# A routing front written as one pipeline over eight blocks, with its parts in another order on three engines

## The reference, cut to what matters

```python
h = layernorm(x) * (1 + ca) + sa
x = x + ga * mamba_stack(h)                     # 4 layers over (8, 512, 128)
h = layernorm(x) * (1 + cb) + sb
normed = h * rsqrt(mean(h*h) + 1e-8) * norm_weight
shared = relu(normed @ sw1 + sb1) @ sw2 + sb2   # 128 -> 512 -> 128
probs = sigmoid(normed @ router_w.T)            # 8 experts
scores, idx = top_k(probs, 2); w = scores / (sum(scores) + 1e-6)
routed = sum over the two chosen e of w_e * (relu(normed @ ew1[e] + eb1[e]) @ ew2[e] + eb2[e])
out = x + gb * (shared + routed)
```

## Time and the profile before

| | us |
|---|---|
| median of 3 runs | 1139.5 (1137.28 to 1139.51) |
| profiled execution, its own time | 1144.36 |
| its span, first to last instruction | 1142.4 |
| Mamba stage, ends with the last add on POOL | at 793.5 |
| `slot(0)` starts | at 808.00 |
| `slot(7)` starts | at 927.79 |
| first matmuls of the experts (transposes) | at 944.83 |
| experts end, sum and output begin | about 1118 |

### The profile page before, as it was taken

The page is one execution under the profiler, slowest core; times in us unless marked ns, Lnnn a source line. Parts: engine busy times, 40 slices in busy tenths (PEclk is TensorE's granted clock), DMA queues, the critical chain, the costliest instruction groups (busy, mean ns, idle before and its releaser), DMA issues.

```text
span 1142.4 us, 20674 instructions
## 1 busy us (share of the span) xinstructions
PE 995.8 (87%) x6136; PEld 557.6 (49%) x6136; DVE 970.0 (85%) x1801; ACT 864.6 (76%) x1636; POOL 675.6 (59%) x853
## 2 busy tenths in 40 slices
PE   5699999999999999999999999985878767999970
PEld 4244454445445444554454455432444436777750
DVE  6679999999999999999999999974788766888865
ACT  4679999899989999999899999983566534556540
POOL 0167767767776777577557656752354451666660
PEclk9789999999999999999999999997889888999995
DMA  5000232223112321100000000000010016766638
GB/s 144 16 12 12 70 133 76 74 75 133 67 68 103 114 72 69 60 3 4 16 10 3 3 5 3 3 3 0 20 38 27 31 38 202 236 227 218 218 114 220
DMA packets 57420, 83.91 MB, mean 73 GB/s; under 512 B 17562, under 2 KB 37664, under 8 KB 57312
## 3 DMA queue, kind: packets, MB, share of 16 engines
q1 hardware_dynamic: 52320, 74.13, 20.3%
q0 software_dynamic: 4992, 8.48, 2.2%
HBM read 44.99 MB, written 37.83 MB: 72 GB/s over the span
## 4 chain that ended last, share of the span: by engine, by line
POOL 40%; issue 28%; PE 18%; DVE 7%; ACT 3%; DMA 2%; SPq 1%; POOLq 1%; DVEq 0%; ACTq 0%
POOL own L1637 6%; POOL dtx L1611 6%; POOL yt L1660 5%; POOL xw L1616 5%; POOL y L1664 5%; PE bank L662 2%; PE bank L663 2%; PE bank L664 2%; POOL WS L1648 2%; PE bank L674 2%; PE bank L676 2%; PE bank L673 2%; POOL h L1652 2%; POOL WS L1646 1%; POOL dt_ L1603 1%
## 5 line engine op out<-in xcount | busy, mean ns | idle before, releaser
L1335 DVE SCALAR_TENSOR_TENSOR cv<-bank,PAR,cv 128x511 f32<-128x511 f32 (+2 forms) x384 | 273.9, 740 | 6.5 <-ACT cv L942 2.8
L1351 DVE SCALAR_TENSOR_TENSOR M<-E,bank 128x512 f32<-128x512 f32 x256 | 168.0, 676 | 21.5 <-ACT E L930 16.1
L1660 POOL TENSOR_TENSOR yt<-yt,ti 128x384 f32<-128x384 f32 x64 | 64.1, 1001 | 194.7 <-DVE ti L1451 194.7
L930 ACT ACTIVATE E<-bank 128x512 f32<-128x512 f32 x256 | 149.0, 596 | 19.1 <-DVE M L1351 18.2
L475 PE MATMUL bank<-hn,WA 128*128 128x512 f32 x256 | 144.6, 647 | 20.7 <-DVE cv L1335 20.2
L1691 POOL DMA_INDIRECT RS<-y,XR x92 | 98.8, 1074 | 78.6 <-DVE y L1548 55.3
L1684 POOL DMA_INDIRECT XS<-stage,IDX x64 | 65.5, 1024 | 79.0 <-DVE run L1310 62.0
L1082 ACT ACTIVATE hr<-bank,W1B 128x512 f32<-128x512 f32 x92 | 63.4, 689 | 56.8 <-PE bank L664 48.9
L543 PE MATMUL bank<-M,dtx 128*32 128x128 f32 x2048 | 82.9, 279 | 14.6 <-DVE o_sb L1370 14.2
L1478 DVE TENSOR_TENSOR hL<-hr,hH 128x512 fp32r<-128x512 f32 x124 | 87.1, 703 | 4.3
L1664 POOL TENSOR_TENSOR y<-yt,zs 128x512 f32<-128x512 f32 x64 | 81.4, 1272 | 5.0
(11 more groups left out here) (244 smaller groups left out, 2610.5 us busy)
## 6 DMA issues: line engine op xcount, KB each, us to landing
XS<-PADT SPq DMA_DIRECT2D x32, 520.0 KB, 4.8
W1B<-WD SPq DMA_DIRECT2D x23, 514.0 KB
W2B<-WD SPq DMA_DIRECT2D x23, 512.5 KB
WD<-WS SPq DMA_DIRECT2D x16, 512.0 KB, 2.9
XR<-XS SPq DMA_DIRECT2D x23, 260.0 KB
RW<-w_in SPq DMA_DIRECT2D x18, 256.0 KB, 4.7
xin<-x_in SPq DMA_DIRECT2D x4, 512.0 KB, 8.3
PC<-p SPq DMA_DIRECT2D x128, 6.0 KB
```

The costliest lines, as they stand in the source:

```text
L930: f(E[i % 2][:, :], bank[2 + i % 2][:, :], ACT.Exp).then_inc(e_a, 1)
L1335: stt(out=cv[t][:, s:L], in0=src[:, 0:L - s], scalar=PAR[:, bass.ds(cw + 3 - s, 1)], in1=cv[t][:, s:L], op0=ALU.mult, op1=ALU.add).then_in ...
L1351: stt(out=M[i % 4][:, :].rearrange("p (n t) -> p n t", n=4), in0=E[i % 2][:, :].rearrange("p (n t) -> p n t", n=4), scalar=1.0, in1=bank[5 ...
L1660: tt(yt[t][:, 128:512], yt[t][:, 128:512], ti[t][:, :], ALU.add).then_inc(fin_p, 1)
```

## The change

`front(n)` becomes `front(i)`, called for i from -3 to 10 on all three engines. A step issues parts of several blocks, each behind a condition that keeps its block number between 0 and 7 and leaves out what the last steps of the Mamba stage already issue (the norm chain of blocks 0 and 1). No arithmetic is added or removed. `rank` is cut into `probability`, `compare`, `ranks` and `choose`; `probability(i + 1)` ends a step and the other three are spread over the next one. POOL and SP are untouched. Of the waits, those of DVE on its own last result move to the head of the next piece. Below is the new order, where every call stands behind its condition (left out here).

```diff
+FRONT = 3
@@ PE @@
+            def front(i):
+                    turn_base(i - 1)
+                    shared_up(i, 0)
+                    mean(i + 2)
+                    shared_up(i, 1)
+                    positions(i)
+                    square_mean_of_m(i + 1)
+                    shared_down(i, 0)
+                    shared_up(i, 2)
+                    shared_up(i, 3)
+                    logits(i + 1)
+                    square_mean_of_h(i + 3)
+                    turn_tokens(i + 1)
+                    shared_down(i, 1)
+                    shared_down(i, 2)
+                    shared_down(i, 3)
+                    variance(i + 2)
-            turn_tokens(0)
-            for n in range(NB):
-                front(n)
-            turn_base(NB - 1)
+            for i in range(-FRONT, NB + FRONT):
+                front(i)
@@ ACT @@
+            def front(i):
+                    root_x(i + 1)
+                    shared_relu(i, 0)
+                    keep_base(i - 1)
+                    square_m(i + 1)
+                    shared_relu(i, 1)
+                    root_m(i + 1)
+                    shared_relu(i, 2)
+                    square_h(i + 3)
+                    shared_relu(i, 3)
+                    exp_logits(i + 1)
+                    square_x(i + 2)
+                    root_h(i + 3)
+                    halve(i + 1)
+                    shared_result(i)
+                    put_tokens(i + 1)
-            put_tokens(0)
-            square_h(2)
@@ DVE @@
-            def rank(n):
+            def probability(n):
+                wait(dve, ex_a, n + 1)
+                r(ts(prx[:, :], pr[:, :], 1.0, None, ALU.add), n, 1)
+                r(nc.vector.reciprocal(pm[:, :], prx[:, :]), n)
+            def compare(n):
+                wait(dve, rt_v, 20 * n + 2)
                 r(tt(pairs(cgt), inner, outer, ALU.is_gt), n)
                 r(tt(pairs(ceq), inner, outer, ALU.is_equal), n, 4)
-                r(tt(pairs(ceq), pairs(ceq), tri, ALU.mult), n, 5)
+                r(tt(pairs(ceq), pairs(ceq), tri, ALU.mult), n)
+            def ranks(n):
+                wait(dve, rt_v, 20 * n + 5)
                 r(tt(cgt[:, :], cgt[:, :], ceq[:, :], ALU.add), n, 6)
+                r(nc.vector.tensor_reduce(rnk[:, :], cgt[:, :].rearrange("p (q f) -> p q f", f=NE), AX.X, ALU.add), n)
+            def choose(n):
+                wait(dve, rt_v, 20 * n + 7)
                 r(ts(m40[:, 0:32], rnk[:, :], 1.5, None, ALU.is_lt), n)
+            def front(i):
+                    compare(i)
+                    add_shared(i - 1)
+                    halve(i)
+                    ranks(i)
+                    add_mamba(i + 2)
+                    choose(i)
+                    modulate(i + 1)
+                    halves(i, 0)
+                    routing_weight(i)
+                    halves(i, 1)
+                    centre(i + 2)
+                    scale(i + 1)
+                    slot(i)
+                    halves(i, 2)
+                    halves(i, 3)
+                    probability(i + 1)
```

More of the change, by code:

```diff
@@ L709, in positions, with shared_up @@
                 ins.then_inc(pos_mm, 1)
-            def front(n):
+            def shared_up(n, t):
                 half = slice((n % 2) * L, (n % 2 + 1) * L)
[L714 to L739, removed]
+                if t == 0:
+                    wait(pe, nh_a, n + 1)
+                    wait(pe, nl_v, n + 1)
+                    if n == 0:
+                        wait(pe, split_p, 4)
+                        wait(pe, ex_a, 1)
+                up(n, t, SW[0], nH[:, half], nL[:, half])
@@ new lines, in shared_down @@
+            def shared_down(n, t):
+                down(n, t, SW[1])
+            def front(i):
+                if 0 <= i - 1 < NB:
+                    turn_base(i - 1)
+                if 0 <= i < NB:
+                    shared_up(i, 0)
+                if 2 <= i + 2 < NB:
+                    mean(i + 2)
+                if 0 <= i < NB:
+                    shared_up(i, 1)
+                if 0 <= i < NB:
+                    positions(i)
+                if 1 <= i + 1 < NB:
+                    square_mean_of_m(i + 1)
+                if 0 <= i < NB:
+                    shared_down(i, 0)
+                if 0 <= i < NB:
+                    shared_up(i, 2)
+                if 0 <= i < NB:
+                    shared_up(i, 3)
+                if 1 <= i + 1 < NB:
+                    logits(i + 1)
+                if 2 <= i + 3 < NB:
+                    square_mean_of_h(i + 3)
+                if 0 <= i + 1 < NB:
+                    turn_tokens(i + 1)
+                if 0 <= i < NB:
+                    shared_down(i, 1)
+                if 0 <= i < NB:
+                    shared_down(i, 2)
+                if 0 <= i < NB:
+                    shared_down(i, 3)
+                if 1 <= i + 2 < NB:
+                    variance(i + 2)
@@ L1104, in keep_base, with shared_relu, shared_result @@
                 f(h[:, n * L:(n + 1) * L], bank[7][:, :], ACT.Copy).then_inc(base_a, 1)
[L1106 to L1125, removed]
-                result(n, PAR2[:, F_B2:F_B2 + 1])
[L1127 to L1132, removed]
+            def shared_relu(n, t):
+                relu(n, t, PAR2[:, F_B1 + t:F_B1 + t + 1])
+            def shared_result(n):
+                result(n, PAR2[:, F_B2:F_B2 + 1])
+            def front(i):
+                if 1 <= i + 1 < NB:
+                    root_x(i + 1)
+                if 0 <= i < NB:
+                    shared_relu(i, 0)
+                if 0 <= i - 1 < NB:
+                    keep_base(i - 1)
+                if 1 <= i + 1 < NB:
+                    square_m(i + 1)
+                if 0 <= i < NB:
+                    shared_relu(i, 1)
+                if 1 <= i + 1 < NB:
+                    root_m(i + 1)
+                if 0 <= i < NB:
+                    shared_relu(i, 2)
+                if 2 <= i + 3 < NB:
+                    square_h(i + 3)
+                if 0 <= i < NB:
+                    shared_relu(i, 3)
+                if 1 <= i + 1 < NB:
+                    exp_logits(i + 1)
+                if 2 <= i + 2 < NB:
+                    square_x(i + 2)
+                if 2 <= i + 3 < NB:
+                    root_h(i + 3)
+                if 1 <= i + 1 < NB:
+                    halve(i + 1)
+                if 0 <= i < NB:
+                    shared_result(i)
+                if 0 <= i + 1 < NB:
+                    put_tokens(i + 1)
             def high_slots(i):
@@ L1153, in _ @@
             act.wait_ge(hup, NB + STEPS)
-            put_tokens(0)
-            square_h(2)
-            for n in range(NB):
-                front(n)
-            keep_base(NB - 1)
+            for i in range(-FRONT, NB + FRONT):
+                front(i)
             for g in range(2):
@@ L1484, in add_shared @@
                 stt(out=xb, in0=es[:, :], scalar=MOD[:, 40 + n:41 + n], in1=xb, op0=ALU.mult, op1=ALU.add).then_inc(fo_v, 1)
[L1486 to L1504, removed]
+            def front(i):
+                if 0 <= i < NB:
+                    compare(i)
+                if 0 <= i - 1 < NB:
+                    add_shared(i - 1)
+                if 1 <= i < NB:
+                    halve(i)
+                if 0 <= i < NB:
+                    ranks(i)
+                if 2 <= i + 2 < NB:
+                    add_mamba(i + 2)
+                if 0 <= i < NB:
+                    choose(i)
+                if 1 <= i + 1 < NB:
+                    modulate(i + 1)
+                if 0 <= i < NB:
+                    halves(i, 0)
+                if 0 <= i < NB:
+                    routing_weight(i)
+                if 0 <= i < NB:
+                    halves(i, 1)
+                if 2 <= i + 2 < NB:
+                    centre(i + 2)
+                if 1 <= i + 1 < NB:
+                    scale(i + 1)
+                if 0 <= i < NB:
+                    slot(i)
+                if 0 <= i < NB:
+                    halves(i, 2)
+                if 0 <= i < NB:
+                    halves(i, 3)
+                if 0 <= i + 1 < NB:
+                    probability(i + 1)
             def t_(ins, own):
```

4 lines of the change are left out of this document (removed).

## The result

The changed kernel takes 1120.38 us (median of 4 runs, 1119.98 to 1120.75) beside 1139.51 us before: a ratio of 0.9831, 95% interval 0.981 to 0.9852, 19.1 us less. The forecast was 1124.6 in a range of 1118 to 1134. In what follows, a "fall" is a stretch in which PE works at the lower of its two clock levels (1.2 GHz in place of 2.4), and a "full" period is one of the first five of the seven; the last two have less of the norm chain to do.

The account below looks back on a forecast made before the run. The prediction took DVE's waits and PE's stretches at 1.2 GHz to bound the front. A full-clock gain of 21.3 us less 6.4 for falls gave 14.9, so 1139.5 becomes 1124.6 us, range 1118 to 1134.

Parts of the forecast that it names:

- The loop: Front, DVE with PE and ACT: 6.0 us from `scale` to `result` plus 8.8 of DVE work, a 14.8 us period.
- DVE's own work: DVE in the front: four waits on its own results, 0.11 each, go, so 14.7 becomes 14.3 us per period.
- The start: Front before `slot(0)`: added work ahead of `choose(0)` and `put_tokens(0)` makes `slot(0)` 1.0 us later.
- The end: Last two of the seven periods: shorter as norm parts run out, 12.3 and 11.2 us.
- At full clock: Seven periods from `slot(0)` to `slot(7)` with PE always at 2.4 GHz: 97.5 us against 119.8.
- The clock term: PE in the front: five falls to the lower clock take back 6.4 us of the gain.
- The price of a fall: PE in the front: about 0.3 us outside the leg from `scale` to `result`, 3.1 if slow over all of it.
- the forecast's own case: Whole kernel: a gain of 10 to 19 us, giving 1120.5 to 1129.5 us, with chance 0.50.
- rival A: PE in the front: the clock stays up and all 21.3 us come, 1118 us; chance 0.17.
- Rival B: Front: falls hit the new loop nearly every period, taking 16 of 21.3 us, about 1134; chance 0.20 for 1129.5 to 1137.
- D: Front tied to POOL's scatters or DVE's own work, so no change, 1139 us; chance 0.07 together with B's end.
- The new POOL queue: POOL in the front: eight scatters and one iota need 10.3 us per block, and POOL just keeps up.

Follow-up runs that it names:

- e2: The changed kernel with `compare` moved from ahead of `add_shared` to behind it on DVE; 1132.2 us, ratio 0.9938 to the kernel before.
- e3: The changed kernel with `square_mean_of_h` ahead of `logits` on PE and `square_h` ahead of `root_m` on ACT; 1117.6 us, ratio 0.9805 to the kernel before.
- e5: The changed kernel without the middle matmul of every shared `up` and `down` in the front; 1119.0 us, ratio 0.9822 to the kernel before.
- e4: The kernel before with seven unused matmuls per block in PE's idle gap ahead of `square_mean_of_h`; 1130.8 us, ratio 0.9921 to the kernel before.
- e9: e3 with four more unused matmuls on PE ahead of `mean`; 1118.7 us, ratio 0.9823 to the kernel before.

## Why the prediction was right, and where a term was off

- **The loop.** The leg from `scale` to `add_shared` was summed as 6.0 and measured 6.11, the period as 14.8 and measured 14.73, DVE's wait in it as 0.5 and measured 0.49. e2 and e3, which lengthen and shorten this loop at constant work, moved the full period to 16.06 and 14.27, so the experiments show that the loop sets the period.
- **DVE's own work** without some self-waits was put at 14.3; e3's period of 14.27 shows it. In the changed kernel the instruction behind the reduction (827.26 to 827.60) starts 0.34 later, without a wait, where one with a wait starts 0.45 later in both kernels. By the page "VectorE: DVE Perf Modes" of the Trainium skill, section "The DRAIN you can't avoid", whose measurement is of eight `tensor_copy`s, the semaphore costs nothing extra, and the floor would be 14.7; e3 went below that, so the trace decides against it for these operations. DVE's busy share between the slots was forecast as about 95% and is 92%: the 14.3 is start-to-start time, of which the profile counts 13.6 as busy.
- **The start**: +1.0 forecast, +0.90 measured. **The end**: 12.3 and 11.2 forecast, 12.50 and 11.25 measured.
- **At full clock** the seven periods were put at 97.5; 98.31 less the one fall (15.64 - 14.73 = 0.91) is 97.4.
- **The clock term was off.** I took five falls at 1.28 us, 6.4 in all; there was one, of 0.91. That is 5.5 us. With this term right the sum would have been a gain of 20.4, beside 20.8 in the profile (without the Mamba part) and 19.1 between the medians; the 1.3 us are no more than the two medians of the changed kernel differ by (1120.4 and 1118.9). It also explains `slot(7)`, forecast for 913 to 914 and found at 903.66: 5.5 are this term, 3.6 the Mamba part. The step that failed was "nearer to the row of before than to no fall, because the gaps stay". In the full periods the gaps did not stay alike: the longest went from 1.87 to 1.18 us. But the last period of the changed kernel has a gap of 1.84, ahead of `turn_base` at 898.09, and a granted clock of 1.00. So the length of the longest gap does not explain it by itself, and why there was one fall and not five stays open.
- **The price of a fall** was off too, which the small number of falls hid. Outside the leg from `scale` to `result` a fall was put at 0.3, and this one, which began outside it, cost 0.91, since relu came 0.56 late and `root_m` 0.16 late for DVE. A fall on the leg in the new order was seen in full in e5's third period: 1.45 us more than its first (15.72 and 14.27), with three matmuls less on the leg, where the term took 3.1 for a leg wholly at the lower clock.
- **Between two cases.** The measured 1120.4 lies just outside the 1120.5 to 1129.5 of the forecast's own case, between it and rival A. "TensorE: Matmul & The Clock Gate", Part 1, of the Trainium skill, on which A rested, agrees with e4 and e9, where added activity kept the clock up (1.00 in place of 0.87 in e4, and in place of e3's 0.98 in e9); in the changed kernel itself one fall was left.
- **Rival B** did not happen in the changed kernel. In e2, the same kernel with a loop 1.3 us longer, six of seven windows have falls, so the margin is small. But they did not land on the leg, as B had it: they began in `up(i, 0)` or at `mean`, and the logits and `square_mean_of_h` behind `scale` took 1.06 and 1.10 us there as in the changed kernel. They cost 4.7 us more than the one fall, where B took 16 in all.
- **D** fell: with POOL busy for 61.80 us between the slots in place of 58.64, the periods shrank by 18%.
- **The new POOL queue** was put at 10.3 us per block. The earlier trace rows give the 1.26 as the length of the first scatter only; that 1.26 is also the step from most scatters to the next (0.96 and a pause of 0.30) was not in the row. In a steady period the queue took 10.8 us of 14.73 and had room. For block 5 it needed 11.65, from 881.68 to 893.33:

```profile
881.68 1.26 POOL L1740 DMA_INDIRECT XS<-stage,IDX  x1 [3.63 <-DVE run L1351]
...
887.26 1.47 POOL L1740 DMA_INDIRECT XS<-stage,IDX  x1 [0.30 <-issue]
889.03 1.47 POOL L1740 DMA_INDIRECT XS<-stage,IDX  x1 [0.30 <-issue]
...
892.16 1.17 POOL L1740 DMA_INDIRECT XS<-stage,IDX  x1 [0.30 <-issue]
893.34 0.16 POOL L1733 IOTA stage<- 128x8 int32 x1
894.19 1.26 POOL L1740 DMA_INDIRECT XS<-stage,IDX  x1 [0.69 <-POOL stage L1733]
```

Block 6 is released by the staging iota in place of `slot`, though no later: 1.78 us after `slot(6)`, where block 5 started 1.77 after `slot(5)`. Block 7 (905.66) starts 2.00 after `slot(7)`, where it was 1.77 before, and that is 0.23 of the +0.32 ahead of the experts. I had said that POOL "just keeps up"; it doesn't quite.

Left open: why a fall comes in this period and not in that. The experiments tell how many there are under a given order, not a rule. The new orders of PE and ACT were not tried apart from each other.

## What to carry to other kernels

When engines hand work to each other in a fixed order, sum each engine's work and every loop of hand-overs that closes over one period: here the longest sum was the period, and a piece of DVE work of some 1.2 us cost 1.33 us more inside the loop than outside it. The orders of the engines belong together: DVE's part of this change alone lost 20 us, and the parts of PE and ACT without DVE's lost 39. A gap of PE can cost time beyond its own wait when it brings the lower clock, and that time can look like a wait of another engine, as `modulate`'s for `root_x` did: nearly half of the gain in the front could be had with seven useless matmuls per block.

## What the runs showed of the hardware that I had not expected

- Useless matmuls in a 1.87 us gap of PE raised the granted clock between the slots from 0.87 to 1.00 and saved 10.2 us of 119.8 (e4).
- Taking 1.8 us of PE work out of each period of 14.7 brought the clock down in three windows instead of one, with gaps of at most 1.4 us in the full period that fell (e5); lengthening the period by 1.33 us, with one more gap of 0.87 us ahead of `up`, in six (e2). The changed kernel had a gap of 1.84 us in a window whose granted clock was 1.00. Small differences decide, and the length of one gap alone does not.
- Most of the indirect DMAs on POOL took 0.96 us and some up to 1.48, in both kernels, so that eight of them with the pauses cost 10.2 to 10.6 us in the kernel before and 10.2 to 11.7 in the changed one. What DVE does meanwhile may be the reason; no run isolated it.
